# Cutting GpSimd's long two-input operations into instructions of 256 columns in a gated cross-attention and FFN kernel

## The chip, the cores and the metric

The kernel runs on one core of a Trainium2 chip. The metric is the device time of one execution in microseconds. TensorE (PE) multiplies and transposes, VectorE (DVE) and ScalarE (ACT) work on SBUF and PSUM, GpSimd (POOL) on SBUF only, and SyncE (SP) issues the DMAs.

## The reference

Four batches of 256 tokens of width 256 attend to a context of 1601 rows (the context is key and value at once, with a mask over its rows), then go through a gated FFN of hidden width 1024 whose matmul inputs are rounded to FP8. Both results are added behind a tanh gate.

```python
# x (4, 256, 256), ctx_2048 (4, 1601, 256), mask (4, 1601)
scores = jnp.einsum('bsd,bmd->bsm', layernorm(x), ctx) * (1 / sqrt(256))
attn = softmax(where(mask, scores, -1e30))
x = x + tanh(g_xattn[0]) * jnp.einsum('bsm,bmd->bsd', attn, ctx)
h = layernorm(x)
act = gelu(qdot(h, w_gating[0])) * qdot(h, w_gating[1])   # qdot: both inputs to float8_e4m3, result bf16
x = x + tanh(g_ffn[0]) * qdot(act, w_linear)
```

## The kernel before

The attention is computed in float32 precision out of two parts: each operand is split into a high part (ScalarE's copy to fp32r, `_hi`) and a residual (`_lo`, the value minus the high part), and TensorE multiplies high by high, high by low and low by high. The context of a batch (`cn`, 13 row tiles of 128 partitions and 256 columns, the last of 65 rows) is handled in NG = 4 groups: three of GT = 4 tiles (1024 columns) and one of the short tile. For the scores the context is transposed through three PSUM banks (`ring`): TensorE fills a bank (`fill`, L580), ScalarE takes the high part (`fill_hi`, L369), VectorE the residual (`fill_lo`, L436), which also frees the bank. Scores are computed by `score` (L595, L600, L601), masked and reduced to a maximum by VectorE (`mask_max`, L446, L452), exponentiated by ScalarE (`exp`, L382), transposed again by way of `ring` (TensorE, L580), split again (L369, L436) and multiplied with the context by `weigh` (L615 high, L619 low). VectorE adds the result to x (`add_attention`, L460 to L469); L463 and L465 are operations of one column with two SBUF inputs.

The context as a value also needs a high and a low part: `chl` holds both side by side in 512 columns a tile. ScalarE writes the high part (`ctx_hi`, L376), and GpSimd the low one (`ctx_lo`, L334): one subtraction a group, 1024 columns for the first three, 65 rows and 256 columns for the fourth. It is signalled by `c_lo`, for which `weigh` and the loads of the context two batches later wait.

The six weight tiles (1024 columns each) are rounded before they are used: VectorE builds a grid out of the exponent bits (`w_grid`, L496 and L497, both from SBUF to SBUF), and GpSimd adds the grid to the weights (L342) and subtracts it again into bf16 (L343), in `round_w`. `link` puts a semaphore wait between those two. `w_ready` is what the next load into the same buffer, the next but one `w_grid` and the FFN's first matmul wait for. GpSimd further computes the masks' bias (`mask_bias`, L311 and L314) and the reciprocal roots of the variances (`first_rstd`, L320, `second_rstd`, L326).

VectorE's normalisation of x is `normed` (L428, two instructions of 256 columns for a batch, in fp32 from SBUF to SBUF), that for the FFN `normed2` (L479). The statistics are L419, L422 and L425.

The order of all this is written out by hand in the strings START, MIDDLE (used for two batches) and END. Each engine goes through the same list and executes those of its steps: Z is `ctx_lo`, I is `round_w`, W `w_grid`, F and Q the roots, B the bias, K `normed`, C, X, T, N the fills of a bank, S `score`, M `mask_max`, E `exp`, V `weigh`, A `add_attention`, U the second statistics, L `normed2`, H and Y the FFN (L654 and L668). Engines meet by semaphores only. SyncE's queue holds the loads in a fixed order, each with its own wait.

Of the kernel before, what the change touches and what calls it, by code (L numbers as in the profile page):

```python
# [5 lines left out]
def gated_cross_attention_ffn(  # L6
# [20 lines left out]
    f32, f32r = mybir.dt.float32, mybir.dt.float32r  # L27
    bf16, f8 = mybir.dt.bfloat16, mybir.dt.float8e4
    u8, u16 = mybir.dt.uint8, mybir.dt.uint16
    ALU = mybir.AluOpType  # L30
    ACT = mybir.ActivationFunctionType

    B, S, D = x.shape
    K = ctx_2048.shape[1]
    HID = w_gating.shape[2]
# [69 lines left out]
    with ExitStack() as stack:  # L105
        def sb(name, shape, dt):
            return stack.enter_context(nc.sbuf_tensor(name, shape, dt))
# [4 lines left out]
        def sem(name):  # L112
            return stack.enter_context(nc.semaphore(name))


        cn = [sb(f"cn{i}", [P, NT, D], f32) for i in range(2)]
        chl = [sb(f"chl{i}", [P, NT, 2 * D], f32r) for i in range(2)]
# [12 lines left out]
        ws = sb("ws", [P, 2, HID], f32)  # L130
        wc = sb("wc", [P, 2, HID], bf16)
        wq = sb("wq", [P, WC, HID], bf16)
# [56 lines left out]
        c_lo = sem("c_lo")  # L189
# [13 lines left out]
        w_ready = sem("w_ready")  # L203
# [8 lines left out]
        def group(g):  # L212
            return (GT * g, min(GT * g + GT, NF), P) if g < NG - 1 else (NF, NT, TAIL)
# [82 lines left out]
        @block.gpsimd  # L296
        def _(pool):
            links = [0]

            def link(ins):  # L300

                links[0] += 1
                ins.then_inc(pool_link, 1)
                pool.wait_ge(pool_link, links[0])

            def mask_bias(b):

                pool.wait_ge(m_in[b % 2], 16 * (b // 2 + 1))
                if b >= 2:
                    pool.wait_ge(masked, 2 * QT * (b - 1))  # L310
                nc.gpsimd.tensor_scalar(bias[:, b % 2, 0:NF * P].rearrange("p (t k) -> p t k", t=NF),  # L311
                                        mrow[:, b % 2, 0:NF * P].rearrange("p (k t) -> p t k", t=NF),
                                        NEG, -NEG, ALU.mult, ALU.add)
                nc.gpsimd.tensor_scalar(bias[:, b % 2, NF * P:K], mrow[:, b % 2, NF * P:K],  # L314
                                        NEG, -NEG, ALU.mult, ALU.add).then_inc(bias_ready, 1)

            def first_rstd(b):
                pool.wait_ge(var_ready, b + 1)
                j = QT * b
                nc.gpsimd.tensor_tensor(rstd[:, j:j + QT], ve[:, j:j + QT], half_pow[:, 0:QT],  # L320
                                        ALU.pow).then_inc(rstd_ready, 1)

            def second_rstd(b):
                pool.wait_ge(var2_ready, QT * (b + 1))
                j = QT * b
                nc.gpsimd.tensor_tensor(rstd2[:, j:j + QT], ve2[:, j:j + QT], half_pow[:, 0:QT],  # L326
                                        ALU.pow).then_inc(rstd2_ready, 1)

            def ctx_lo(b, g):
                t0, t1, parts = group(g)  # L330
                pool.wait_ge(c_hi, NG * b + g + 1)
                if g == NG - 1:
                    pool.wait_ge(c_lo, NG * b + g)
                nc.gpsimd.tensor_tensor(chl[b % 2][0:parts, t0:t1, D:2 * D], cn[b % 2][0:parts, t0:t1, :],  # L334
                                        chl[b % 2][0:parts, t0:t1, 0:D].bitcast(f32), ALU.subtract).then_inc(c_lo, 1)
                if g == NG - 1:
                    pool.wait_ge(c_lo, NG * (b + 1))

            def round_w(i):

                pool.wait_ge(wc_ready, i + 1)
                link(nc.gpsimd.tensor_tensor(ws[:, i % 2, :], ws[:, i % 2, :], wc[:, i % 2, :], ALU.add))  # L342
                nc.gpsimd.tensor_tensor(wq[:, i, :], ws[:, i % 2, :], wc[:, i % 2, :], ALU.subtract).then_inc(w_ready, 1)  # L343

            link(nc.gpsimd.memset(ident[:], 0.0))
            nc.gpsimd.affine_select(out=ident[:], in_=ident[:], compare_op=ALU.not_equal, fill=1.0, base=0,
                                    pattern=[[-1, P]], channel_multiplier=1).then_inc(ident_ready, 1)
            link(nc.gpsimd.memset(half_pow[:], -0.5))
            pool.wait_ge(ident_ready, 1)
            nc.gpsimd.tensor_copy(ident16[:], ident[:]).then_inc(ident_ready, 1)  # L350
            for s in order:
                if s[0] == "F":
                    first_rstd(s[1])
                elif s[0] == "B":
                    mask_bias(s[1])
                elif s[0] == "Z":
                    ctx_lo(s[1], s[2])
                elif s[0] == "I":
                    round_w(s[1])
                elif s[0] == "Q":  # L360
                    second_rstd(s[1])
# [351 lines left out]
```

## Time and profile before

| what | before |
|---|---|
| median of 3 runs | 150.0 us (149.98 to 152.47) |
| profiled execution: span, first to last instruction | 149.9 us |
| its own time, the span with what lies around it | 150.0 us |
| TensorE busy | 130.0 us, 786 matmuls |
| VectorE busy | 126.9 us, 255 instructions |
| GpSimd busy | 74.8 us, 52 instructions |
| ScalarE busy | 71.2 us, 131 instructions |

How to read it: a row of a timeline gives the start in the span, the duration, engine, source line and operation, what is written from what, the shapes and the count, and in brackets how long the engine sat idle before it and what ended that. A row with xN merges N like neighbours. The duration of a VectorE or GpSimd instruction includes a wait for a resource inside the engine, since only waits on semaphores are shown as idle time. Rows of the chain of waits have start, duration, engine, tile and line. PEclk is TensorE's granted clock as a share of the full one.

### The profile page before, as it was taken

To read this page: it belongs to the slowest core of one execution; us is meant where nothing else is said; L and a number is where in the kernel's file an instruction comes from. 1 tells how busy PE (TensorE), PEld (TensorE's weight loads), DVE (VectorE), ACT (ScalarE), POOL (GpSimd) and SP (SyncE) were. 2 spreads that over 40 slices of the span, in tenths; PEclk is the share of its full clock that TensorE was granted. 3 is DMA by queue.
4 is the path that set the end of the run, shared out by engine and by line. 5 is a ranking of instruction groups with operands and counts; after the bars stand their busy time and mean duration, and the time that the engine had idled before them with its cause. 6 is when DMAs were issued, how large, how long until landed. Compare 5 with 4: busy or idle time off the path is not lost.

```text
span 149.9 us, 2277 instructions
## 1 busy us (share of the span) xinstructions
PE 130.0 (87%) x786; PEld 106.3 (71%) x786; DVE 126.9 (85%) x255; ACT 71.2 (47%) x131; POOL 74.8 (50%) x52
## 2 busy tenths in 40 slices
PE   7389967998769799983999799939999899999992
PEld 5179847996757699873887798828889777344781
DVE  1458999999999999899699998996899696988752
ACT  3075319799225466920254559410541592557300
POOL 2106892769999905379997010599990100100000
PEclk9978999999999999999699999995999999999999
DMA  1599930059300591000301300000000000000133
GB/s 41 219 376 385 377 145 4 0 165 350 124 0 0 179 413 42 4 0 17 123 0 7 133 0 4 2 0 0 0 4 0 2 0 0 0 4 0 35 115 130
DMA packets 6754, 12.75 MB, mean 85 GB/s; under 512 B 852, under 2 KB 4696, under 8 KB 6744
## 3 DMA queue, kind: packets, MB, share of 16 engines
q1 hardware_dynamic: 6456, 12.62, 24.2%
q8 instruction: 6, 0.10, 0.3%
q10 hardware_dynamic: 288, 0.00, 0.1%
q14 instruction: 4, 0.03, 0.1%
HBM read 11.57 MB, written 1.05 MB: 84 GB/s over the span
## 4 chain that ended last, share of the span: by engine, by line
PE 50%; DVE 36%; DMA 5%; issue 4%; ACT 2%; SPq 1%; DVEq 0%
PE ring L580 12%; PE pv L615 11%; PE scores L654 7%; DVE act L428 6%; PE pv L619 6%; DVE wc L497 5%; DMA cn<-in_ctx_dram 5%; DVE wc L496 5%; DVE pT_lo L436 4%; PE ring L668 4%; DVE sp L446 3%; PE scores L600 3%; PE scores L601 3%; PE scores L595 3%; DVE cT_lo L436 2%
## 5 line engine op out<-in xcount | busy, mean ns | idle before, releaser
L334 POOL TENSOR_TENSOR chl<-cn,chl 128x1024 fp32r<-128x1024 f32 (+1 forms) x16 | 31.9, 2006 | 4.0 <-ACT chl L376 3.8
L369 ACT ACTIVATE pT_hi<-ring 128x512 fp32r<-128x512 f32 (+1 forms) x32 | 15.7, 514 | 36.3 <-PE ring L580 36.3
L615 PE MATMUL pv<-chl,pT_hi 128*128 128x512 f32 (+1 forms) x104 | 32.5, 427 | 0.0
L600 PE MATMUL scores<-cT_lo,xT_hi 128*128 128x512 f32 (+2 forms) x64 | 21.9, 350 | 6.6 <-DVE cT_lo L436 6.6
L601 PE MATMUL scores<-cT_hi,xT_lo 128*128 128x512 f32 (+2 forms) x64 | 21.7, 346 | 0.0
L436 DVE TENSOR_TENSOR pT_lo<-ring,pT_hi 128x512 fp32r<-128x512 f32 (+1 forms) x32 | 18.1, 582 | 3.7 <-ACT pT_hi L369 3.7
L619 PEld LDWEIGHTS pv<-chl,pT_lo 128*128 128x128 f32 (+1 forms) x104 | 16.9, 200 | 5.8 <-issue 1.9
L615 PEld LDWEIGHTS pv<-chl,pT_hi 128*128 128x128 f32 (+1 forms) x104 | 19.0, 199 | 2.7
L619 PE MATMUL pv<-chl,pT_lo 128*128 128x256 f32 (+1 forms) x104 | 18.3, 296 | 2.7 <-DVE pT_lo L436 2.7
L382 ACT ACTIVATE sp<-sp,nb 128x1024 f32<-128x1024 f32 (+1 forms) x16 | 15.4, 962 | 9.7 <-DVE nb L452 9.7
L580 PE MATMUL ring<-ident,sp 128*128 128x128 f32 (+1 forms) x104 | 16.5, 285 | 2.8 <-ACT sp L382 2.8
L595 PE MATMUL scores<-cT_hi,xT_hi 128*128 128x512 f32 (+2 forms) x64 | 18.7, 373 | 0.0
L342 POOL TENSOR_TENSOR ws<-ws,wc 128x1024 f32<-128x1024 f32 x6 | 13.0, 2160 | 11.4 <-DVE wc L497 11.4
L436 DVE TENSOR_TENSOR cT_lo<-ring,cT_hi 128x512 fp32r<-128x512 f32 (+1 forms) x28 | 16.7, 626 | 2.3 <-ACT cT_hi L369 2.0
L600 PEld LDWEIGHTS scores<-cT_lo,xT_hi 128*128 128x128 f32 x64 | 12.0, 188 | 8.6 <-DVE cT_lo L436 7.2
L580 PE MATMUL ring<-ident,cn 128*128 128x128 f32 (+1 forms) x104 | 15.4, 285 | 3.0 <-DMA cn<-in_ctx_dram 2.9
L369 ACT ACTIVATE cT_hi<-ring 128x512 fp32r<-128x512 f32 (+1 forms) x28 | 14.5, 550 | 6.4 <-PE ring L580 6.2
L580 PEld LDWEIGHTS ring<-ident,cn 128*128 128x128 f32 (+1 forms) x104 | 13.0, 151 | 4.2 <-issue 3.3
L580 PEld LDWEIGHTS ring<-ident,sp 128*128 128x128 f32 (+1 forms) x104 | 13.1, 147 | 4.0 <-issue 3.3
L326 POOL TENSOR_TENSOR rstd<-ve,half_pow 128x2 f32<-128x2 f32 x4 | 2.8, 698 | 26.1 <-DVE ve L425 26.1
L446 DVE CUSTOM_DVE_ANT_0 sp<-scores,bias 128x1024 f32<-128x1024 f32 (+1 forms) x16 | 15.7, 981 | 0.1
L376 ACT ACTIVATE chl<-cn 128x1024 fp32r<-128x1024 f32 (+1 forms) x16 | 14.3, 899 | 1.2 <-DMA cn<-in_ctx_dram 1.2
(58 smaller groups left out, 203.9 us busy)
## 6 DMA issues: line engine op xcount, KB each, us to landing
cn<-in_ctx_dram SPq DMA_DIRECT2D x12, 512.0 KB, 6.5
ws<-in_L_ffn_w_gating_dram SPq DMA_DIRECT2D x4, 512.0 KB, 7.2
ws<-in_L_ffn_w_linear_dram SPq DMA_DIRECT2D x2, 512.0 KB, 3.8
out_dram<-xs SPq DMA_DIRECT2D x8, 128.0 KB, 1.7
mrow<-in_mask_BxS_bk_dram SPq DMA_DIRECT2D x4, 200.1 KB, 6.8
xs<-in_x_dram SPq DMA_DIRECT2D x1, 768.0 KB, 9.2
cn<-in_ctx_dram SPq DMA_DIRECT2D x4, 65.0 KB
xs<-in_x_dram SPq DMA_DIRECT2D x1, 256.0 KB, 4.2
```

Of the source, the lines that this page charges most:

```text
L334: nc.gpsimd.tensor_tensor(chl[b % 2][0:parts, t0:t1, D:2 * D], cn[b % 2][0:parts, t0:t1, :], chl[b % 2][0:parts, t0:t1, 0:D].bitcast(f32), ...
L369: nc.scalar.activation(dst, bank_view(f, size), ACT.Copy).then_inc(hi_ready, 1)
L376: nc.scalar.activation(chl[b % 2][0:parts, t0:t1, 0:D], cn[b % 2][0:parts, t0:t1, :], ACT.Copy).then_inc(c_hi, 1)
L382: nc.scalar.activation(sp[:, j % 2, cols], sp[:, j % 2, cols], ACT.Exp, bias=nb[:, j:j + 1], scale=SCALE, accum_out=rs[:, j, h:h + 1]).the ...
L436: nc.vector.tensor_tensor(dst, bank_view(f, size), hi.bitcast(f32), ALU.subtract).then_inc(freed, 1)
L446: nc.vector.tensor_tensor_reduce(out=sp[:, j % 2, cols], in0=banks[:, at_col:at_col + cols.stop - cols.start], in1=bias[:, b % 2, cols], s ...
L580: last = nc.tensor.transpose(dst, src, ident[0:parts, 0:parts])
L595: nc.tensor.matmul(dst, xT_hi[:, j, k, :], cT_hi[:, k, cols], start=(k == 0), stop=False)
L600: nc.tensor.matmul(dst, xT_hi[:, j, k, :], cT_lo[:, k, cols], start=False, stop=False)
L601: last = nc.tensor.matmul(dst, xT_lo[:, j, k, :], cT_hi[:, k, cols], start=False, stop=(k == KD - 1))
L615: return nc.tensor.matmul(pv[:, :], pT_hi[0:parts, t, :], chl[b % 2][0:parts, t, :], start=(t == 0), stop=(t == NT - 1))
L619: nc.tensor.matmul(pv[:, 0:D], pT_lo[0:parts, t, :], chl[b % 2][0:parts, t, 0:D], start=False, stop=False)
```

## The change

The long subtraction of a context group is issued as one instruction a tile, so four of 256 columns for a full group (the short group keeps its one). Each of the two operations on a weight tile is issued as four of 256 columns: first the four additions, then the wait of `link`, then the four subtractions. The last piece of each set carries the signal that the whole instruction carried. Order of the steps, waits and data are as before.

```diff
             def ctx_lo(b, g):
...
-                nc.gpsimd.tensor_tensor(chl[b % 2][0:parts, t0:t1, D:2 * D], cn[b % 2][0:parts, t0:t1, :],
-                                        chl[b % 2][0:parts, t0:t1, 0:D].bitcast(f32), ALU.subtract).then_inc(c_lo, 1)
+                for t in range(t0, t1):
+                    last = nc.gpsimd.tensor_tensor(chl[b % 2][0:parts, t, D:2 * D], cn[b % 2][0:parts, t, :],
+                                                   chl[b % 2][0:parts, t, 0:D].bitcast(f32), ALU.subtract)
+                last.then_inc(c_lo, 1)
                 if g == NG - 1:
                     pool.wait_ge(c_lo, NG * (b + 1))
 
             def round_w(i):
 
                 pool.wait_ge(wc_ready, i + 1)
-                link(nc.gpsimd.tensor_tensor(ws[:, i % 2, :], ws[:, i % 2, :], wc[:, i % 2, :], ALU.add))
-                nc.gpsimd.tensor_tensor(wq[:, i, :], ws[:, i % 2, :], wc[:, i % 2, :], ALU.subtract).then_inc(w_ready, 1)
+                quarters = [slice(c, c + HID // 4) for c in range(0, HID, HID // 4)]
+                for c in quarters:
+                    last = nc.gpsimd.tensor_tensor(ws[:, i % 2, c], ws[:, i % 2, c], wc[:, i % 2, c], ALU.add)
+                link(last)
+                for c in quarters:
+                    last = nc.gpsimd.tensor_tensor(wq[:, i, c], ws[:, i % 2, c], wc[:, i % 2, c], ALU.subtract)
+                last.then_inc(w_ready, 1)
```

## Rows read from the trace of the kernel before

**Rows 1.** The page: busy time, share of the span and instructions of each engine
```profile
PE 130.0 (87%) x786; PEld 106.3 (71%) x786; DVE 126.9 (85%) x255; ACT 71.2 (47%) x131; POOL 74.8 (50%) x52
```

**Rows 2.** Timeline of TensorE: the instructions before which it sat idle
```profile
23.29 0.63 PE L580 MATMUL ring<-ident,sp 128*128 128x128 f32 x4 [2.24 <-ACT sp L382]
...
38.38 0.37 PE L600 MATMUL scores<-cT_lo,xT_hi 128*128 128x288 f32 x1 [1.41 <-DVE cT_lo L436]
...
43.01 0.74 PE L619 MATMUL pv<-chl,pT_lo 128*128 128x256 f32 x4 [1.24 <-DVE pT_lo L436]
...
49.67 0.36 PE L619 MATMUL pv<-chl,pT_lo 65*128 65x256 f32 x1 [1.18 <-DVE pT_lo L436]
...
69.80 0.41 PE L600 MATMUL scores<-cT_lo,xT_hi 128*128 128x290 f32 x1 [2.72 <-DVE cT_lo L436]
...
83.26 0.66 PE L580 MATMUL ring<-ident,act 128*128 128x128 f32 x4 [0.84 <-DVE pT_lo L436]
...
100.54 0.40 PE L600 MATMUL scores<-cT_lo,xT_hi 128*128 128x290 f32 x1 [2.43 <-DVE cT_lo L436]
```

**Rows 3.** One stretch with engines' busy times and PEclk; then the chain of waits
```profile
70.00:75.00 5.00, 5.00 (x23) 4.48 (x23) 3.64 (x10) 1.10 (x3) 5.00 (x3) 0.66 0.33 105
...
71.39 1.71 PE pv L615 x4
...
87.12 0.94 PE pv L615 x4
...
101.34 1.65 PE pv L615 x4
```

**Rows 4.** Timeline of VectorE: instructions that read SBUF alone, free and stretched
```profile
6.99 0.73 DVE L428 TENSOR_SCALAR act<-xs,mv,rstd 128x256 f32<-128x256 f32 x2 [0.83 <-POOL rstd L320]
...
17.41 3.54 DVE L428 TENSOR_SCALAR act<-xs,mv,rstd 128x256 f32<-128x256 f32 x2
...
39.07 2.54 DVE L497 TENSOR_SCALAR wc<-wc 128x1024 bf16<-128x1024 bf16 x1
...
46.13 3.20 DVE L428 TENSOR_SCALAR act<-xs,mv,rstd 128x256 f32<-128x256 f32 x2
...
49.95 0.16 DVE L465 TENSOR_TENSOR fo<-ri,vt 128x1 f32<-128x1 f32 x1
...
63.36 0.68 DVE L496 TENSOR_SCALAR wc<-ws 128x1024 uint16<-128x1024 uint16 x1
64.07 0.43 DVE L497 TENSOR_SCALAR wc<-wc 128x1024 bf16<-128x1024 bf16 x1
...
65.02 2.26 DVE L496 TENSOR_SCALAR wc<-ws 128x1024 uint16<-128x1024 uint16 x1
67.31 2.23 DVE L497 TENSOR_SCALAR wc<-wc 128x1024 bf16<-128x1024 bf16 x1
...
75.74 3.03 DVE L428 TENSOR_SCALAR act<-xs,mv,rstd 128x256 f32<-128x256 f32 x2
...
109.57 1.99 DVE L465 TENSOR_TENSOR fo<-ri,vt 128x1 f32<-128x1 f32 x1
```

**Rows 5.** Timeline of GpSimd: long instructions beside them, and one of 256 columns
```profile
41.29 3.43 POOL L334 TENSOR_TENSOR chl<-cn,chl 128x1024 fp32r<-128x1024 f32 x2
...
66.81 2.45 POOL L343 TENSOR_TENSOR wq<-ws,wc 128x1024 bf16<-128x1024 f32 x1
...
80.80 0.76 POOL L334 TENSOR_TENSOR chl<-cn,chl 65x256 fp32r<-65x256 f32 x1
```

**Rows 6.** Timelines of GpSimd, VectorE and TensorE: results of GpSimd and their use
```profile
56.42 0.69 POOL L326 TENSOR_TENSOR rstd<-ve,half_pow 128x2 f32<-128x2 f32 x1 [3.79 <-DVE ve L425]
...
60.76 0.76 DVE L479 TENSOR_SCALAR xn<-xs,mv,rstd 128x256 fp8e4<-128x256 f32 x2
...
109.39 2.15 POOL L343 TENSOR_TENSOR wq<-ws,wc 128x1024 bf16<-128x1024 f32 x1
...
120.10 1.89 PE L654 MATMUL scores<-x2T,wq 128*128 128x512 fp8e4 x8
```

## The prediction

> **What bounds the kernel now.** I read the page's busy times first: TensorE 130.0 us, VectorE 126.9 and GpSimd 74.8 of a span of 149.9 [rows 1]. No engine is idle enough to call the others hidden, so the question is who makes TensorE wait. Next I read TensorE's timeline for its gaps. Behind the opening loads, and up to the last stage, eight gaps stand out: 2.24, 1.41, 1.24, 1.18, 2.72, 0.33, 0.84 and 2.43 us, 12.4 us in all; all but one end with a residual written by VectorE, and the first with an exponential that itself waited for VectorE's maximum (the smallest is not shown) [rows 2]. After the two longest, TensorE's granted clock was down: 0.66 over 70 to 75 us, and four matmuls of the attention product took 1.71 and 1.65 us where the same four take 0.94 at full clock; with the residual product and the transposes beside them this costs about 1.5 us the first time and 1.1 the second, 2.6 us [rows 3]. So about 15 us of TensorE's time hang on VectorE's lateness.
>
> Then I read VectorE's timeline for instructions of one form and two durations. A pair of normalising operations (L428) takes 0.73 us in one place and 3.54, 3.20 and 3.03 in others; the exponent mask of the weights (L496) 0.68 or 2.26; the grid operation (L497) 0.43 or 2.54 and 2.23; the one-column product with 1/sum (L465) 0.16 or 1.99, and 2.00 at 34.01 us [rows 4]. There are fifteen such stretched entries, the first and the last of them at 17.41 and 109.57 us, and their excess over the free form sums to 25.4 us. Each ends just after a GpSimd instruction ends: L497 of 67.31 ends at 69.54, GpSimd's L343 ends at 66.81 + 2.45 = 69.26; L497 of 39.07 ends at 41.61, GpSimd's next subtraction of ctx begins at 41.29 [rows 4, 5]. VectorE's instructions with a PSUM input (L436, 0.68 us) never stretch, whatever GpSimd does. So the stretched ones wait for something that a running GpSimd instruction holds to its end, and the hold is as long as that instruction: about 2.15 us for a weight operation of 1024 columns [rows 6], 2.4 for a ctx subtraction, of which two in a row begin 2.34 us apart, at 38.95 and 41.29 [rows 5].
>
> **The change, part by part.**
> *Removed:* 12 long subtractions of ctx and 12 weight operations, each one hold of 2.1 to 2.5 us. *Added:* 48 + 48 instructions of 256 columns. The four short subtractions (65 rows, 256 columns) are already of this size and stay; such a one takes 0.76 us with waits on both sides [rows 5]. Signals still come from the last piece, so no consumer may start earlier.
>
> *Price of a piece.* The floor is a quarter of the whole: 0.60 us of 2.4 and 0.54 of 2.15, adding nothing. The ceiling is the 65-row form, 0.76 less the 0.05 to 0.08 us by which neighbours in GpSimd's timeline overlap: 0.7, so four make 2.8, +0.4 on a ctx group and +0.65 on a weight operation. I take a third to a half of it, +0.25 us a group, since part of the 0.76 us is the start and the drain that neighbours overlap. That is 24 x 0.25 = 6 us more GpSimd time (range 0 to 12.6), on an engine busy for half of the span.
> The Trainium skill (GPSIMD Engine Reference, Performance versus the Vector engine) gives 4497 ns for a two-input add of 2048 columns, which is 2.2 ns a column; with this case's 2.15 us for 1024 that leaves no fixed part at all, and by the page the cut would add about nothing.
>
> *What VectorE gets back.* A contending instruction now waits for the end of a piece, 0.3 us on average if it comes at random, and up to 0.6 if it follows another contender and GpSimd has taken the next piece in between. By places on TensorE's list of gaps [rows 2, 4]:
> - Gap of 2.24 (ends at 23.29): the L428 pair of 17.41 becomes 0.73 + 0.3 + 0.6 = 1.6 us instead of 3.54, so both pass before the mask operation of batch 1 (uncut) takes its turn; the maximum behind it and its exponential come 1.9 earlier. Recovered: 1.7.
> - Gaps of 1.41, 1.24, 1.18: the causes are L465 at 34.01 (excess 1.84, now about 0.4), L497 at 39.07 (2.11, now 0.5) and the L428 pair at 46.13 (2.47, now 0.9). VectorE gains 4.6 there and has to make up 3.8. Recovered: all 3.8.
> - Gap of 2.72: W2, the cast and W3 run in one string from 63.36; L496 of 65.02 and L497 of 67.31 lose 1.58 and 1.80 now, 0.3 and 0.5 afterwards. VectorE would reach the residual that TensorE waits for at about 67.2 instead of 69.54; TensorE is ready at 67.08. Recovered: 2.4, and with a gap of 0.3 instead of 2.7 the clock's 1.5.
> - Gaps of 0.33 and 0.84: the L428 pair of 75.74 (excess 2.30, then 0.9) and an L463 behind it. Recovered: 1.2.
> - Gap of 2.43: the same string a batch later. Recovered: 2.1, and 1.1 of clock.
> Sum: 1.7 + 3.8 + 2.4 + 1.5 + 1.2 + 2.1 + 1.1 = 13.8 us. Behind 101 us I count nothing: L463 and L465 at 107 to 111 us lose 3.8 us now (the last row of the group is one of them), but TensorE works through them without a gap.
> Once TensorE no longer waits for these, it is itself what is late: it would be busy in nearly all of 21 to 117 us. I take 1.8 us off for small new waits (eleven pieces of 0.1 to 0.3 us where VectorE, still busy about 102 of 138 us, meets a piece just before TensorE wants its result). Gain 12.0.
>
> *What hides the slower GpSimd.* Its results have slack now. In the stretch that runs without a break from 31.6 to 52.6 us it has seven long instructions; behind it, it sat idle 3.79 us until the second variance came (56.42), and the result was used only at 60.76, 3.65 us after it was there [rows 6]: 7.4 us of cover. The stretch starts about 2.3 us earlier, its consumers come 5.5 us earlier, and it grows by 7 x 0.25 = 1.8: 5.0 of the 7.4 are used. At the ceiling (7 x 0.53 = 3.7) 6.9 are used: just enough. The last weight is ready at 111.54 and TensorE's first hidden matmul is at 120.10: 8.6 us of cover, of which 3.2 (earlier consumer) and 1.8 to 3.7 (growth) go [rows 6]. DMAs of the weights and of ctx wait on these signals in SP's queue; they land over 6 us ahead of their use and lose 2 to 4 of that.
>
> The profiled execution has a span of 149.9 us, and some 0.1 us around it makes the 150.0 of the runs' median; 150.0 - 12.0 = 138.0.
>
> **Rivals.**
> *A. No hand-over between pieces (slower).* Four pieces stand in GpSimd's queue with nothing between them. If VectorE gets its turn only when that queue runs dry or meets a wait, it waits for the whole group as before, and the group is longer by 0.25 to 0.5 us. Thirteen of the stretched entries lie on TensorE's path, and some pairs pay twice: 13 x 0.25 = 3.3, 153.3 us (up to 156). It decides from the point where VectorE's mean wait exceeds the present one, 1.7 us an entry. For it: the neighbours overlap in the timeline, so the next one has begun when the first ends. The Trainium skill (GPSIMD Engine Reference, Instruction dispatch) says that completion doesn't hold back the next Pool instruction, and that each of its cores goes on as soon as its own share is done; by that rule alone the hold might never open between queued pieces. Against it: between the subtractions of 38.95 and 41.29, whose waits had long been met (GpSimd shows no idle time between them), L497 came in and ended at 41.61; the same at 69.22, at the end of L343 [rows 4, 5]. Only an already met wait stood between them.
> *B. GpSimd becomes the bound.* If a piece costs 0.8 us or more (hand-overs on top: L343 took 2.45 instead of 2.15 when VectorE stood in between [rows 5]), seven long instructions grow by 7 us, 4 to 5 us beyond the cover in each of the three full stretches; perhaps half reaches TensorE: 138 + 6.5 = 144.5.
> *C. Half the gaps come back in another form*, because VectorE's order, with its own 102 us of work, or ScalarE's exponentials hold TensorE at the same places: 150 - 6 = 144.
> *D. The hold is not the instruction's length* but something else of GpSimd's activity: no gain, 150 to 151.
>
> **How the numbers follow.** Forecast 0.74, B 0.09, C 0.08, A 0.06, D 0.03. The forecast's own range is 134.5 (all 12.4 + 2.6 recovered) to 141.5; with B and C the range is 134.3 to 145.5, which leaves out A, D and the far ends. A measurement of this kernel can tell about 2%, 3 us. Faster by over 2%: forecast, nearly all of B and C, 0.89; within 2%: 0.04; slower: 0.07.
>
> **What would show it.** Right: L428 pairs at 0.8 to 1.8 us, L496 and L497 under 1.1, L463 and L465 under 0.8; VectorE's busy time near 108 us instead of 126.9; TensorE's gaps of 2.72 and 2.43 below 0.6 and the granted clock at 1.00 in both places; GpSimd busy 78 to 86 us; the last weight ready before the first hidden matmul. Wrong: stretched entries still of 2 us and more (A or D), rows in which TensorE or VectorE wait for GpSimd's rstd or weights (B), or gaps of TensorE of over 1 us behind ScalarE (C).

## The result, and the profile after

The changed kernel takes 140.8 us (median; 139.6 to 142.1) against 150.2 for the kernel before, a ratio of 0.931 (0.920 to 0.943). Repeated later it gave 0.934 (0.926 to 0.942). The forecast was 138.0, in a range of 134.3 to 145.5, faster. Times here and below are medians of all runs, ratios and intervals those of the runs in the faster of a kernel's two states alone, so that a ratio need not be the quotient of two medians.

One number of the forecast has to be put right first: a run's time is its span plus 1.8 us (142.13 and 140.3 for the profiled execution of the changed kernel), not plus 0.1. The profiled execution of before, with its span of 149.9 us, was thus by estimate one of about 151.7. Spans are compared with spans from here on: 149.9 to 140.3, a gain of 9.6 where 12.0 was forecast. The profiled execution of the repeat (span 139.4) has the same waits.

The page after, busy times and granted clock. Line numbers of the changed kernel are 7 higher behind the change, so L428 is now L435, L463 L470, L465 L472, L479 L486, L496 L503, L497 L504:

```profile
PE 128.2 (91%) x786; PEld 105.0 (75%) x786; DVE 110.5 (79%) x255; ACT 71.7 (51%) x131; POOL 86.1 (61%) x124
...
PEclk9999999999999999999999999999999599999999
```

VectorE does the same 255 instructions in 16.4 us less, GpSimd does its work in 11.3 us more [rows 1]. The clock no longer falls at 70 and 100 us, but has a new dip near 110.

VectorE's timeline after, the stretched instructions of [rows 4] and the L465 of 34.01 us, and at the end the first hold that stayed long:

```profile
17.81 1.67 DVE L435 TENSOR_SCALAR act<-xs,mv,rstd 128x256 f32<-128x256 f32 x2
...
31.89 0.33 DVE L472 TENSOR_TENSOR fo<-ri,vt 128x1 f32<-128x1 f32 x1
...
36.08 0.84 DVE L504 TENSOR_SCALAR wc<-wc 128x1024 bf16<-128x1024 bf16 x1
...
41.43 1.15 DVE L435 TENSOR_SCALAR act<-xs,mv,rstd 128x256 f32<-128x256 f32 x2
...
59.62 0.69 DVE L503 TENSOR_SCALAR wc<-ws 128x1024 uint16<-128x1024 uint16 x1
60.34 2.35 DVE L504 TENSOR_SCALAR wc<-wc 128x1024 bf16<-128x1024 bf16 x1
```

What took 3.54, 2.00, 2.54 and 3.20 us takes 1.67, 0.33, 0.84 and 1.15. The last row is the exception that proves useful below: 2.35 us beside a GpSimd instruction that the change left whole. Summed over L435, L470, L472, L486, L503 and L504 (count times mean less the free duration, from the groups by line), the excess went from 25.5 to 8.5 us.

GpSimd's groups by line, and its timeline beside those rows and in the last attention stage:

```profile
L335 POOL TENSOR_TENSOR chl<-cn,chl 128x256 fp32r<-128x256 f32 x48 | 34.6, 759 | 0.5 <-ACT chl L383 0.4
L346 POOL TENSOR_TENSOR ws<-ws,wc 128x256 f32<-128x256 f32 x24 | 16.1, 706 | 4.9 <-DVE wc L504 4.8
```
```profile
46.23 2.58 POOL L346 TENSOR_TENSOR ws<-ws,wc 128x256 f32<-128x256 f32 x4
...
54.95 0.69 POOL L326 TENSOR_TENSOR rstd<-ve,half_pow 128x2 f32<-128x2 f32 x1
59.77 2.65 POOL L311 TENSOR_SCALAR bias<-mrow 128x1536 bf16<-128x1536 uint8 x1 [4.12 <-DMA mrow<-in_mask_BxS_bk_dram]
...
92.67 8.42 POOL L335 TENSOR_TENSOR chl<-cn,chl 128x256 fp32r<-128x256 f32 x12
101.04 2.59 POOL L346 TENSOR_TENSOR ws<-ws,wc 128x256 f32<-128x256 f32 x4
103.70 2.57 POOL L349 TENSOR_TENSOR wq<-ws,wc 128x256 bf16<-128x256 f32 x4
106.23 0.72 POOL L335 TENSOR_TENSOR chl<-cn,chl 65x256 fp32r<-65x256 f32 x1
107.03 0.71 POOL L326 TENSOR_TENSOR rstd<-ve,half_pow 128x2 f32<-128x2 f32 x1
```

The row of 92.67 holds three ctx groups of four pieces, so one takes 8.42 / 3 = 2.81 us instead of 2.4, a set on the weights 2.58 instead of 2.15 [rows 5, 6]. The root of 54.95 has no idle time before it (3.79 us before the change), that of 107.03 neither. VectorE's timeline shows who waits for the roots:

```profile
55.68 0.74 DVE L486 TENSOR_SCALAR xn<-xs,mv,rstd 128x256 fp8e4<-128x256 f32 x2 [0.85 <-POOL rstd L326]
...
83.29 0.73 DVE L486 TENSOR_SCALAR xn<-xs,mv,rstd 128x256 fp8e4<-128x256 f32 x2 [2.00 <-POOL rstd L326]
...
101.22 0.15 DVE L432 TENSOR_SCALAR ve<-mv 128x1 f32<-128x1 f32 x1
...
107.77 0.73 DVE L486 TENSOR_SCALAR xn<-xs,mv,rstd 128x256 fp8e4<-128x256 f32 x2 [4.33 <-POOL rstd L326]
```

The third variance was written at 101.37 and its root began 5.66 us later, because GpSimd first had a weight step and a short ctx group in its order. TensorE's timeline after, for comparison with [rows 2, 3, 6]:

```profile
21.83 0.63 PE L587 MATMUL ring<-ident,sp 128*128 128x128 f32 x4 [0.39 <-ACT sp L389]
...
35.35 0.29 PE L607 MATMUL scores<-cT_lo,xT_hi 128*128 128x288 f32 x1
...
38.51 0.63 PE L626 MATMUL pv<-chl,pT_lo 128*128 128x256 f32 x4
...
62.95 0.40 PE L607 MATMUL scores<-cT_lo,xT_hi 128*128 128x290 f32 x1 [1.54 <-DVE cT_lo L443]
...
73.26 0.60 PE L587 MATMUL ring<-ident,act 128*128 128x128 f32 x4
...
89.22 0.32 PE L607 MATMUL scores<-cT_lo,xT_hi 128*128 128x290 f32 x1
...
97.66 0.40 PE L607 MATMUL scores<-cT_lo,xT_hi 128*128 128x512 f32 x1
...
107.01 0.38 PE L626 MATMUL pv<-chl,pT_lo 65*128 65x256 f32 x1 [1.44 <-ACT sp L389]
...
108.61 0.58 PE L585 MATMUL ring<-ident,xn 128*128 128x128 bf16 x4 [0.55 <-issue]
108.99 3.40 PE L661 MATMUL scores<-x2T,wq 128*128 128x512 fp8e4 x8
```

The same instructions stand in [rows 2], so the changed kernel's lead can be read off, beside the running sum of the forecast's terms up to that gap:

| instruction | before | after | lead | forecast |
|---|---|---|---|---|
| transposes of `sp` | 23.29 | 21.83 | 1.5 | 1.7 |
| L600, 288 columns | 38.38 | 35.35 | 3.0 | 3.1 |
| L619 | 43.01 | 38.51 | 4.5 | 4.4 |
| L600, 290 columns | 69.80 | 62.95 | 6.9 | 7.9 |
| transposes of `act` | 83.26 | 73.26 | 10.0 | 10.6 |
| L600, 290 columns | 100.54 | 89.22 | 11.3 | 12.7 |
| L600, 512 columns | 110.62 | 97.66 | 13.0 | 13.8 |
| first hidden matmuls | 120.10 | 108.99 | 11.1 | 13.8 |
| last instruction | 147.31 | 137.71 | 9.6 | 13.8, less 1.8 |

Up to 98 us the lead grows almost as forecast. Then 3.4 us are lost again, in three parts of about 1.4, 0.5 and 1.5 us. TensorE stands for 1.44 us before the short group's product at 107.01. Its row names ScalarE, whose last instruction ended at 106.95, but so did GpSimd's short ctx subtraction (106.23 + 0.72), which is what this product reads. The weight load of the same product, and the repeat's matmul, name GpSimd (weight load of the change, then matmul of the repeat):

```profile
107.00 0.19 PEld L626 LDWEIGHTS pv<-chl,pT_lo 65*128 65x128 f32 x1 [1.68 <-POOL chl L335]
```
```profile
106.18 0.38 PE L626 MATMUL pv<-chl,pT_lo 65*128 65x256 f32 x1 [1.44 <-POOL chl L335]
```

The second part is 0.55 us before 108.61, where TensorE waits for the `xn` that VectorE could write only after the late root. The third is that the eight hidden matmuls at 108.99 take 3.40 us (1.89 before, [rows 6]), at a granted clock of 0.76 over 106 to 113 us; here is that stretch of seven us:

```profile
106.00:113.00 7.00, 5.45 (x22) 3.04 (x23) 4.98 (x15) 4.01 (x7) 1.66 (x3) 0.76 0.00 0
```

### The profile page after: what moved, and what is told of

It is laid out like the page before. It is cut to its first block, busy times and chain, and to the rows that moved or that the text cites. A ratio compares the mean times of both kernels' runs of the same rounds, so it can differ in the third digit from the quotient of the medians.

```text
span 140.3 us, 2349 instructions
## 1 busy us (share of the span) xinstructions
PE 128.2 (91%) x786; PEld 105.0 (75%) x786; DVE 110.5 (79%) x255; ACT 71.7 (51%) x131; POOL 86.1 (61%) x124
## 4 chain that ended last, share of the span: by engine, by line
PE 64%; POOL 16%; DMA 9%; issue 3%; DVE 3%; ACT 2%; SPq 1%; POOLq 0%
PE ring L587 14%; PE pv L622 12%; PE scores L661 9%; POOL chl L335 7%; PE pv L626 6%; PE scores L602 5%; PE scores L608 5%; PE scores L607 5%; DMA cn<-in_ctx_dram 5%; DMA mrow<-in_mask_BxS_bk_dram 4%; PE ring L675 4%; POOL ws L346 4%; POOL wq L349 3%; POOL bias L311 2%; ACT sp L389 1%
## 5 line engine op out<-in xcount | busy, mean ns | idle before, releaser
L335 POOL TENSOR_TENSOR chl<-cn,chl 128x256 fp32r<-128x256 f32 (+1 forms) x52 | 37.5, 757 | 0.8 <-ACT chl L383 0.4
L622 PE MATMUL pv<-chl,pT_hi 128*128 128x512 f32 (+1 forms) x104 | 30.8, 409 | 0.0
L622 PEld LDWEIGHTS pv<-chl,pT_hi 128*128 128x128 f32 (+1 forms) x104 | 18.1, 189 | 2.7 <-issue 0.3
L346 POOL TENSOR_TENSOR ws<-ws,wc 128x256 f32<-128x256 f32 x24 | 16.1, 706 | 4.9 <-DVE wc L504 4.8
L626 PEld LDWEIGHTS pv<-chl,pT_lo 128*128 128x128 f32 (+1 forms) x104 | 16.0, 189 | 4.2 <-POOL chl L335 2.0
L602 PE MATMUL scores<-cT_hi,xT_hi 128*128 128x512 f32 (+2 forms) x64 | 18.8, 375 | 0.0
L587 PE MATMUL ring<-ident,cn 128*128 128x128 f32 (+1 forms) x104 | 16.1, 297 | 2.8 <-DMA cn<-in_ctx_dram 2.8
L626 PE MATMUL pv<-chl,pT_lo 128*128 128x256 f32 (+1 forms) x104 | 17.2, 285 | 1.5 <-ACT sp L389 1.4
L587 PE MATMUL ring<-ident,sp 128*128 128x128 f32 (+1 forms) x104 | 15.5, 273 | 0.4 <-ACT sp L389 0.4
L349 POOL TENSOR_TENSOR wq<-ws,wc 128x256 bf16<-128x256 f32 x24 | 15.5, 676 | 0.5
L311 POOL TENSOR_SCALAR bias<-mrow 128x1536 bf16<-128x1536 uint8 x4 | 9.6, 2397 | 8.7 <-DMA mrow<-in_mask_BxS_bk_dram 8.5
```

The lines of the kernel that those rows point to most:

```text
L335: last = nc.gpsimd.tensor_tensor(chl[b % 2][0:parts, t, D:2 * D], cn[b % 2][0:parts, t, :], chl[b % 2][0:parts, t, 0:D].bitcast(f32), ALU. ...
L346: last = nc.gpsimd.tensor_tensor(ws[:, i % 2, c], ws[:, i % 2, c], wc[:, i % 2, c], ALU.add)
L349: last = nc.gpsimd.tensor_tensor(wq[:, i, c], ws[:, i % 2, c], wc[:, i % 2, c], ALU.subtract)
L587: last = nc.tensor.transpose(dst, src, ident[0:parts, 0:parts])
L602: nc.tensor.matmul(dst, xT_hi[:, j, k, :], cT_hi[:, k, cols], start=(k == 0), stop=False)
L622: return nc.tensor.matmul(pv[:, :], pT_hi[0:parts, t, :], chl[b % 2][0:parts, t, :], start=(t == 0), stop=(t == NT - 1))
```

## The experiments

The theory after the result has two parts: (1) an instruction of VectorE with its inputs in SBUF waits for the end of GpSimd's running instruction, and gets in between two pieces; (2) what is missing from the forecast was lost because GpSimd, 11 us slower, is late with what stands last in its order. The rivals: the gain comes from something other than the length of a hold; the loss lies with ScalarE or in VectorE's own order.

### One half of the change at a time

```diff
# ctx_only: round_w as before, ctx_lo cut
# weights_only: ctx_lo as before, round_w cut
```

> Only the ctx subtractions are cut; the weight operations stay whole. Theory (a VectorE instruction with its inputs in SBUF waits to the end of the running GpSimd instruction, and this alone is what the cut shortens): in the kernel before, ctx subtractions account for about 4.8 us of the 25.4 us of excess (part of the pairs at 17.41 and 75.74, 22.85, 39.07), so VectorE's busy time falls by 4 to 6 us to about 122 and the time to 145 to 148 us. Entries under the weight operations stay at 2 us and more. Rival (what counts is the total number or length of GpSimd's work, or its alternation with VectorE in general): half of the gain, about 145, with the entries under weight operations shorter too.

> Only the weight operations are cut. Theory: they account for some 18 of 25.4 us of excess and stand before both of TensorE's longest gaps, so most of the gain is here: 141 to 144 us, VectorE busy 113 to 116, the entries at ctx subtractions (39.07 before) still 2 us. GpSimd's work is 2.7 us longer a batch pair less than in the full change, so it may even be as fast as the full change. Rival (both halves matter alike): about 145.

| | time (us) | ratio | span | VectorE busy | excess |
|---|---|---|---|---|---|
| ctx_only | 146.6 | 0.968 (0.959 to 0.977) | 143.2 | 118.3 | 16.9 |
| weights_only | 142.2 | 0.947 (0.939 to 0.955) | 139.8 | 118.8 | 16.4 |
| both (the change) | 140.8 | 0.931 (0.920 to 0.943) | 140.3 | 110.5 | 8.5 |

Both times fall in the ranges of the theory, and the entries shown stay long only where the instructions beside them stayed whole. Under whole weight operations (ctx_only) the pair of 65 us stays long, and under whole ctx subtractions (weights_only) L497's counterpart does:

```profile
61.20 2.25 DVE L498 TENSOR_SCALAR wc<-ws 128x1024 uint16<-128x1024 uint16 x1
63.49 2.22 DVE L499 TENSOR_SCALAR wc<-wc 128x1024 bf16<-128x1024 bf16 x1
```
```profile
35.85 2.49 DVE L502 TENSOR_SCALAR wc<-wc 128x1024 bf16<-128x1024 bf16 x1
```

The split of the excess was forecast wrongly. Either half leaves some 16.5 us of it, not 20 and 7, and VectorE's busy time is 118.3 and 118.8 us, not about 122 and 113 to 116. Probably VectorE, when it comes earlier, meets other GpSimd instructions than before; this was not followed up. The weights are still worth more in time, since their holds stand in front of TensorE's longest gaps: in ctx_only the gaps before L602's 290 columns are 3.63 and 2.41 us, in weights_only the first is 1.55 us and the second is gone.

### Pieces of 512 columns

```diff
-for t in range(t0, t1): ... [t, ...]        # 256 columns
+for t in range(t0, t1, 2): ... [t:min(t + 2, t1), ...]  # 512 columns
-quarters = [slice(c, c + HID // 4) for c in range(0, HID, HID // 4)]
+quarters = [slice(c, c + HID // 2) for c in range(0, HID, HID // 2)]
```

> The changed kernel with pieces of 512 columns in place of 256. Theory (VectorE's wait scales with the piece, GpSimd's overhead with their number): a piece takes 1.2 to 1.3 us, VectorE's excess is about 13 us (8 in the changed kernel, 25 before), GpSimd's busy time about 79 to 80 (86 and 75), and the two effects pull against each other: 140 to 142 us. Rival A of the prediction (hand-over only at the end of a set of pieces) would have VectorE's excess independent of the size of the piece; if only GpSimd's lateness mattered, 512 columns would beat 256 by 1 us or more.

Measured: 143.1 us, 0.946 (0.936 to 0.955), where 140 to 142 was expected. VectorE's excess is 17.6 us, more than the 13 expected, and GpSimd's busy time 79.0. The interval overlaps that of the repeated change (0.926 to 0.942), so 256 columns are not shown to be faster than 512. The hold follows the size of the piece: the excess is 25.5, 17.6 and 8.5 us for 1024, 512 and 256 columns. GpSimd's price follows the number: 74.8, 79.0 and 86.1 us. The groups by line of that kernel:

```profile
L336 POOL TENSOR_TENSOR chl<-cn,chl 128x512 fp32r<-128x512 f32 x24 | 30.3, 1295 | 3.6 <-ACT chl L384 3.5
L347 POOL TENSOR_TENSOR ws<-ws,wc 128x512 f32<-128x512 f32 x12 | 14.6, 1235 | 8.7 <-DVE wc L505 8.6
```

Taken over three sizes, both the prediction's rival A (hand-over only at the end of a set) and its rival D (the hold is not the length) would have left the excess as it was; they fall for these operations.

### Where the end of the forecast went

```diff
# roots_first, GpSimd's own order only
+mine = list(order)
+for q, before in ((0, ("B", 2)), (1, ("I", 3)), (2, ("I", 5))):
+    mine.remove(("Q", q))
+    mine.insert(mine.index(before), ("Q", q))
```

> The changed kernel with three of GpSimd's reciprocal roots moved ahead in its own order: Q0 before the mask operation B2, Q1 before the weight step I3, Q2 before I5. Theory (the part of the forecast that did not come was lost because VectorE waits for these roots: 0.85, 2.00 and 4.33 us idle before L486, and the clock fell behind the last): the waits vanish, TensorE's granted clock stays at 1.00 near 110 us, and the time falls by 2 to 3.5 us, to 137 to 139. Rival (the tail is held by ScalarE's exponentials and by VectorE's own order): within 0.7 us of the changed kernel, about 140.8.

Measured: 142.3 us, 0.944 (0.935 to 0.953): no gain, the theory's number missed. The waits of VectorE for the roots are gone, but TensorE now waits for GpSimd's short ctx groups for longer, 2.78 us where its weight load waited 0.31, and 3.06 instead of 1.44, and the granted clock was 0.55 over 107 to 114 us:

```profile
82.18 0.39 PE L630 MATMUL pv<-chl,pT_lo 65*128 65x256 f32 x1 [2.78 <-POOL chl L335]
```
```profile
108.65 0.58 PE L630 MATMUL pv<-chl,pT_lo 65*128 65x256 f32 x1 [3.06 <-POOL chl L335]
```

The short ctx groups stand behind the weight steps, and with the root moved ahead of them they come still later. The order had only handed the delay to another consumer; so the fault is GpSimd's backlog, not this one wait. (2) holds in its mechanism, but not in the repair.

```diff
# mask_early, in SyncE's queue
             load_mask(2)
+            load_mask(3)
...
             load_ctx(3)
-            load_mask(3)
# order_fix: mask_early, and in GpSimd's order
+for late, before in ((("Q", 0), ("B", 2)), (("Z", 2, 3), ("I", 3)),
+                     (("Z", 3, 3), ("I", 5)), (("Q", 2), ("I", 5))):
+    mine.remove(late)
+    mine.insert(mine.index(before), late)
```

> The changed kernel with the load of batch 3's mask moved ahead of the weight loads 2 and 3 and the ctx load 3 in SyncE's queue. In the changed kernel GpSimd sat idle 4.12 us for that mask (59.77), then ran without a break to 83.26 with the root Q1 at its end, for which VectorE waited 2.00 us, and the uncut mask operation held L504 for 2.35 us. Theory (GpSimd is late, and part of it by this detour): its operations come about 4 us earlier from there on, L486 no longer waits at 83, the 1.54 us gap of TensorE goes; 1.5 to 3 us less than the changed kernel, 138 to 139.5. Rival (the detour is covered elsewhere): no difference, 140.8.

> mask_early, and GpSimd's own order changed: the root Q0 ahead of mask operation B2, the short ctx groups of batches 2 and 3 ahead of the weight steps I3 and I5, and the root Q2 ahead of I5. roots_first had moved roots alone, and TensorE then stood 2.78 and 3.06 us for the short ctx groups behind them. Theory (GpSimd's queue is late by some us in each batch, and what is last in it is waited for): nothing short of the weights is last any more, no engine waits over 1 us for GpSimd, granted clock 1.00 to the end; 136 to 138. Rival (the loss is in the FFN's start, whose matmuls need the last weights): TensorE waits for L349 at 105 to 108 us instead, 139 to 140.

> The kernel before (whole operations) with the load and GpSimd's order changed as in order_fix. Theory: there GpSimd is not late, but holds VectorE; nothing is gained: 149 to 151.5. Rival (the order alone is worth something in either kernel): 147 or less.

| | time (us) | ratio |
|---|---|---|
| the change | 140.8; 141.3 when repeated | 0.931; 0.934 (0.926 to 0.942) |
| mask_early | 139.6 | 0.920 (0.912 to 0.927) |
| order_fix | 139.1 | 0.914 (0.907 to 0.922) |
| old_order_fix | 152.6 | 0.994 (0.987 to 1.001) |

mask_early's gain is at the edge of what the intervals separate (0.912 to 0.927 against 0.926 to 0.942); order_fix lies clear of the change's repeated run, though not quite of its first (0.920 to 0.943). Each ratio is taken against the kernel before in its own group of runs. In the kernel with whole operations the same edits are worth nothing. That alone does not show that the lateness is a product of the cut, since there the edits also put L479 under long instructions: its excess rose from 0.3 to 4.1 us and could hide a small gain. More direct is that in the kernel before GpSimd sat idle ahead of each of the first three roots, 3.79 us [rows 6], 6.07 and 3.95 us; here is the third:

```profile
116.17 0.71 POOL L326 TENSOR_TENSOR rstd<-ve,half_pow 128x2 f32<-128x2 f32 x1 [3.95 <-DVE ve L425]
```

The source of the 4.12 us before 59.77 is now shown too: the load of batch 3's mask stood in SyncE's queue behind loads that wait for GpSimd's own signals. With it moved, GpSimd waits for no mask but the first. Yet the third root came only 1.1 us earlier (105.90 instead of 107.03), not 4: GpSimd next waited 2.92 us for VectorE's grid. The 1.54 us gap went, but the mask operation, now earlier, stretched L486's pair to 2.78 us, and TensorE stood for 2.25 us before 58.52 instead.

In order_fix the rival's wait has come, and at the size that it gave:

```profile
105.82 2.98 PE L665 MATMUL scores<-x2T,wq 128*128 128x512 fp8e4 x8 [2.00 <-POOL wq L349]
```

The last rounded weights are now what is late: TensorE stands for 2.00 us, and the clock falls behind it, to 0.76 over 103 to 110 us (eight matmuls in 2.98 us instead of 1.89). GpSimd is the bound of the end of the attention at pieces of 256 columns.

The fall of the clock does not follow from such a wait alone. In mask_early TensorE stood for 1.34 and 0.55 us at this place, in order_fix_cut below for 2.01 us, and both kept a granted clock of 1.00 and their 1.89 and 1.90 us for the eight matmuls. So 1.1 to 1.5 us of the difference between any two profiled executions can be the clock's, with the same waits.

### The uncut mask operation

```diff
# order_fix_cut: order_fix, and the mask's 12 tiles in four sets of 3 (views shortened)
+for t in range(0, NF, 3):
+    nc.gpsimd.tensor_scalar(bias_view[:, t:t + 3, :], mrow_view[:, t:t + 3, :], NEG, -NEG, ALU.mult, ALU.add)
```

> order_fix with the mask operation (1536 columns, 2.3 us) cut into four of 384 columns too. In order_fix one L474 beside such an operation still takes over 2 us and TensorE has a gap of 1.74 at 61.64. Theory (the hold is that of any long GpSimd instruction): that entry falls below 0.9, the gap closes, 0.5 to 2 us less than order_fix: 136 to 138. Rival (GpSimd is the bound there and four pieces cost it 0.3 us each): no gain or 1 us slower.

Measured: 137.9 us, 0.916 (0.910 to 0.922), against 0.914 for order_fix: medians 1.2 us apart, intervals on top of each other. The long entry beside the mask operation did go. VectorE's timeline of order_fix, then of order_fix_cut:

```profile
54.59 2.19 DVE L474 TENSOR_TENSOR rt<-rs 128x1 f32<-128x1 f32 x1
```
```profile
55.30 0.14 DVE L475 TENSOR_TENSOR rt<-rs 128x1 f32<-128x1 f32 x1
```

But TensorE's gap at 61.6 us only shrank from 1.74 to 1.42, and the wait for the weights stayed (2.01 us). One hold of 2.05 us went, and between 53.8 and 61.4 us several VectorE instructions take longer instead, each beside short pieces: L491's pair 1.41 us instead of 0.94, L477 0.56 instead of 0.16, L508 1.13 instead of 0.68. GpSimd's busy time rose from 86.8 to 89.8. In the two profiled executions the hidden matmuls start at 105.82 and 105.84 us; the 1.6 us by which the second is shorter lie behind that point, 1.1 of them in the clock. Whether this last step gains anything is open.

### Without the long operations

```diff
# left_out: the kernel before, 2 columns a tile instead of 256, 2 of 1024 for the weights
-nc.gpsimd.tensor_tensor(chl[...][..., D:2 * D], cn[...], chl[...][..., 0:D].bitcast(f32), ALU.subtract)
+nc.gpsimd.tensor_tensor(chl[...][..., D:D + 2], cn[...][..., 0:2], chl[...][..., 0:2].bitcast(f32), ALU.subtract)
# and GpSimd clears chl's low halves and wq once
# left_out_2: the clearing at other places, left_out_3: the same in pieces of 256 columns
```

> The kernel before with GpSimd's two kinds of long operations done on 2 columns only (the low part of ctx as value is left at zero but for 2 columns a tile, the rounded weights likewise), signals and order kept. It shows the ceiling: no long holds but the four mask operations. Theory: VectorE busy falls by 22 to 24 us to 103 to 105, no entry over 0.7 us but beside a mask operation, time 134 to 137. Rival (VectorE's stretched entries have another cause than GpSimd's running instruction): VectorE stays near 125 us and the time near 150.

> As left_out, with the three clearing operations moved to places where GpSimd sits idle (in left_out they delayed a reciprocal root and TensorE stood still for 6.06 us before 16.05). Theory: the 6 us come off, 134 to 135 us, which is the ceiling for any way of cutting GpSimd's operations; the forecast of 138.0 was within it. Rival (TensorE's later work absorbs it, and about 140 is the floor of this order): 138 to 140.

> As left_out_2, with the clearing cut into pieces of 256 columns. In left_out_2 the clearing of the weights (5.22 us, writes only) held VectorE's L503 for 5.73 us and the next one L504 for 3.05, and TensorE stood for 6.55 us; from there to the end TensorE had no gap, and gained 6.1 us on order_fix. Theory (a running GpSimd instruction of any kind holds such a VectorE instruction, and nothing else stands in TensorE's way): no entry over 0.9 us but beside the uncut mask operations, span 131 to 133, time 133 to 135. Rival (TensorE's unbroken run was owed to the long stop, which let the others get ahead): 137 or more.

Measured: 140.1, 144.0 and 140.8 us (the last with four runs at 140.8, 135.7, 140.8 and 141.0). None of them gave the ceiling that it was made for (133 to 137 us were expected), since each time GpSimd's clearing stopped VectorE. What they do show is this: in left_out TensorE has one gap of 6.06 us before 16.05, and from there to the FFN none that the timeline marks; without that gap its span of 138.2 would be 132, and its time 134. That is an estimate. The nearest measured run is that of 135.7 us (span 133.8), which was not the profiled one, so that why it was 5 us shorter than its three fellows stays open. By these two numbers some 5 to 7 us more than the change's gain lie in GpSimd's operations, in holds and in lateness together.

## Why the prediction was right, and where it missed

- **What bounds the kernel.** Right. VectorE's lateness made TensorE's gaps, and the gaps went when the holds got shorter; both low-clock stretches behind them went too. Of the 12.4 us of gaps, 1.54 + 0.39 are left; new ones of 0.98, 1.44 and 0.55 us came behind GpSimd's late results.
- **What VectorE gets back.** The sum of the terms was 13.8 us, and the lead reached 13.0. The one term that was too large is the 2.72 us gap: 1.54 stayed. There L504 was held for 2.35 us by the mask operation, which the forecast had not looked at; that operation came 4 us late itself, for want of its load.
- **Price of a piece.** "+0.25 us a group" was too low: 0.41 on a ctx group and 0.43 on a set of weights, 11.3 us in all instead of 6. On a ctx group that is the forecast's ceiling (+0.4, from the row of 256 columns less the overlap), which should have been taken as it stood, and on a weight operation two thirds of it (+0.65). Neither the discount for what neighbours overlap nor the reading by which a cut adds about nothing held: every extra piece cost about 0.14 us.
- **What hides the slower GpSimd.** This step failed. It examined two consumers (the first root of the FFN's normalisation and the last weights) and took them for all. In GpSimd's order the short ctx group, and behind it the second and the third root, stand behind a weight step. VectorE waited 2.00 and 4.33 us for these roots. TensorE lost 3.4 us of its lead behind 98 us: 1.44 waiting for the short ctx group, 0.55 behind the root, 1.5 to the clock. GpSimd's last stretch without a break, of seven long operations and the short group, grew from 16.9 us (95.32 to 112.22) to 20.1 (86.85 to 106.95), by 3.2 and not by 7 x 0.25 = 1.8. The mask's load, which waits in SyncE's queue behind GpSimd's own signals, was on none of the lists. "They land over 6 us ahead of their use" held for weights and ctx alone.
- **The allowance of 1.8 us** for small new waits stood for this loss of 3.4 by luck, not by reason: there were no eleven small waits.
- **Rivals.** B, GpSimd as the bound, came true in part: its waits, at about half of its price (3.4 of 6.5 us). C did not show: the 1.44 us before 107.01, which the profile puts down to ScalarE, were GpSimd's short ctx group, and are not there in order_fix. A and D fell with the 512-column kernel, for the two-input operations.
- **Time and span.** 138.0 rested on 0.1 us around the span; it is 1.8, and 12.0 us off 150.2 would have been 138.2 all the same.

The Trainium skill (SBUF — State Buffer, Who interferes with whom) describes what the rows show: the port pair that VectorE and GpSimd share is held for a whole instruction, and the second one blocks. For two-input operations the traces agree at each of three sizes of piece (excess 25.5, 17.6 and 8.5 us); the clearing operations below do not all fit as simply.

## What to carry to other kernels

When an instruction of one engine has two durations in one trace, look for what the other engine was executing at its end; if the hold ends with that instruction, cutting the instruction can cut the wait (it did here for two-input operations, but not for all clearing operations, see below), and the price is the fixed part of each piece (here about 0.14 us for every extra one). Before cutting, list every consumer of the engine that becomes slower, its DMA triggers included, and compute the cover of each; those that stand behind a long step in its order are the ones that pay. Look at the weight load's row as well as the matmul's before you believe whose delay a wait is. And when moving one late result forward only makes the next one late, it is the backlog that has to be shortened.

## What was not expected of the hardware

Two things, both from the clearing operations of the left_out kernels. GpSimd instructions that only write hold VectorE as well. In left_out_2 (GpSimd's timeline, then VectorE's) the clearing of 5.22 us held L503 to its end, and the one behind it L504:

```profile
29.67 5.22 POOL L358 MEMSET wq<- 128x6144 bf16 x1
34.95 3.30 POOL L359 MEMSET chl<- 128x3328 f32 x1
```
```profile
29.70 5.73 DVE L503 TENSOR_SCALAR wc<-ws 128x1024 uint16<-128x1024 uint16 x1
35.47 3.05 DVE L504 TENSOR_SCALAR wc<-wc 128x1024 bf16<-128x1024 bf16 x1
```

The second is that pieces did not always let VectorE in. In left_out_3 GpSimd cleared `chl` in 26 instructions of 256 columns with nothing between them, and a VectorE instruction that came with the first of them ended only after the last of them, which ended at 13.70 us:

```profile
7.05 6.65 POOL L358 MEMSET chl<- 128x256 f32 x26
```
```profile
7.13 6.71 DVE L440 TENSOR_SCALAR act<-xs,mv,rstd 128x256 f32<-128x256 f32 x1 [0.84 <-POOL rstd L320]
```

That is the prediction's rival A, for clearing operations. Yet in the same kernel 24 pieces that cleared `wq` (bf16, from 34.93 on) let L508 and L509 through at 34.96 and 35.82 in 0.83 and 0.49 us, and two-input operations of one column at 37.75 and 38.12 took their free 0.14 and 0.16. What decides between the two (the type, the operation, or who asks first) was not tried and stays open. The Trainium skill's rule (same section) that a two-input VectorE operation contends only with a GpSimd operation that reads SBUF agrees with those last two.
